# A shared ring of three PSUM bank pairs for attention scores and their maxima

## The reference

```python
x = x + attention(layernorm(x))          # x: 2 x 512 x 512, 32 heads of 16
scores = q @ k.T / sqrt(16)              # 64 (batch, head) pairs of 512 x 512
out = softmax(scores) @ v                # per head
attention = concat(out) @ w_o.T
x = x + experts(layernorm(x))            # top 2 of 8 experts, 512 -> 800 -> 512
```

## Time and profile before

| | us |
|---|---|
| median of three runs | 637.14 (635.68 to 637.60) |
| the profiled execution | 642.03 |
| its span, first to last instruction | 640.30 |
| QKV projection and start, of the span | 0 to about 98 |
| attention steps 0 to 15 and the last PV | about 98 to 291 |
| rest of the output projection, norm, router, experts | about 291 to 640 |

### The profile page before, as it was taken

How to read it: one execution, slowest core, us unless ns; L and a number is a source line. 1 busy time by engine, 2 the same in 40 slices (tenths; PEclk the granted TensorE clock), 3 DMA queues, 4 the chain that set the end, 5 groups by cost and what they waited for, 6 DMA issues and landing times.

```text
span 640.3 us, 10494 instructions
## 1 busy us (share of the span) xinstructions
PE 587.1 (92%) x3585; PEld 434.8 (68%) x3585; DVE 385.6 (60%) x689; ACT 329.5 (51%) x481; POOL 121.0 (19%) x137
## 2 busy tenths in 40 slices
PE   2999999979999999999954999999999999998993
PEld 2886663334333333323753999999999999998982
DVE  6715657958999999614546682837465555647140
ACT  5222116846777777862215464737464646565330
POOL 5000111000101101101004003324150607060312
PEclk9899997968999999999855999999999999999898
DMA  8180336764756620043742555666666574843213
GB/s 316 61 98 1 50 50 84 107 70 71 99 69 93 85 79 18 13 150 116 303 179 70 212 182 160 180 203 165 213 161 228 108 282 76 312 70 120 25 14 38
DMA packets 29497, 78.88 MB, mean 123 GB/s; under 512 B 8490, under 2 KB 8746, under 8 KB 24859
## 3 DMA queue, kind: packets, MB, share of 16 engines
q1 hardware_dynamic: 24474, 68.84, 40.0%
q0 software_dynamic: 4992, 9.64, 8.8%
HBM read 58.64 MB, written 9.80 MB: 107 GB/s over the span
## 4 chain that ended last, share of the span: by engine, by line
PE 45%; issue 28%; POOL 9%; DVE 7%; ACT 4%; DMA 3%; SPq 2%; POOLq 1%; ACTq 0%
PE ps_o L590 9%; PE ps L609 6%; PE ps L578 5%; PE ps L579 4%; PE ps L580 4%; DVE neg_max L1106 4%; POOL out L540 4%; PE ps L665 3%; PE ps_m L609 3%; POOL xn L522 3%; PE ps L621 2%; PE ps_o L729 2%; ACT probs_t L934 2%; SPq L357 1%; DMA rec_row<-sum_rec 1%
## 5 line engine op out<-in xcount | busy, mean ns | idle before, releaser
L934 ACT ACTIVATE probs_t<-ps 128x1024 f32<-128x1024 f32 x128 | 124.0, 1023 | 44.4 <-PE ps L621 43.1
L578 PE MATMUL ps<-xgT_hi,w_hi 128*128 128x294 f32 (+1 forms) x416 | 127.0, 305 | 5.4 <-DVE xgT_lo L1282 2.9
L580 PE MATMUL ps<-xgT_hi,w_lo 128*128 128x294 f32 (+1 forms) x416 | 126.3, 304 | 0.0
L579 PE MATMUL ps<-xgT_lo,w_hi 128*128 128x294 f32 (+1 forms) x416 | 125.5, 302 | 0.0
L1106 DVE TENSOR_REDUCE neg_max<-ps 128x1 f32<-128x512 f32 x171 | 111.7, 684 | 13.5 <-PE ps L609 11.4
L1295 DVE TENSOR_TENSOR act<-gate,ps 128x294 f32<-128x294 f32 x48 | 22.1, 461 | 105.4 <-PE ps L580 86.8
L578 PEld LDWEIGHTS ps<-xgT_hi,w_hi 128*128 128x128 f32 (+1 forms) x416 | 79.0, 190 | 5.9 <-DVE xgT_lo L1282 3.2
L579 PEld LDWEIGHTS ps<-xgT_lo,w_hi 128*128 128x128 f32 (+1 forms) x416 | 78.7, 189 | 0.0
L580 PEld LDWEIGHTS ps<-xgT_hi,w_lo 128*128 128x128 f32 (+1 forms) x416 | 78.4, 188 | 0.0
L609 PE MATMUL ps<-k_stack,q_stack 48*128 48x512 f32 x171 | 74.9, 479 | 2.9 <-issue 0.3
L590 PE MATMUL ps_o<-probs_t,v_ones 128*32 128x512 f32 x512 | 72.3, 639 | 0.3 <-ACT probs_t L934 0.3
(11 more groups left out here) (249 smaller groups left out, 960.2 us busy)
## 6 DMA issues: line engine op xcount, KB each, us to landing
w_sb<-w SPq DMA_DIRECT2D x18, 1024.0 KB
w_sb<-w SPq DMA_DIRECT2D x9, 1536.0 KB
w_sb<-w SPq DMA_DIRECT2D x9, 1152.0 KB
q_stack<-q_hi SPq DMA_DIRECT2D x32, 128.0 KB, 5.1
k_stack<-k_hi SPq DMA_DIRECT2D x32, 128.0 KB, 4.8
q_stack<-q_lo SPq DMA_DIRECT2D x16, 128.0 KB, 4.9
k_stack<-k_lo SPq DMA_DIRECT2D x16, 128.0 KB, 5.9
q_hi<-o_norm SPq DMA_DIRECT2D x16, 128.0 KB, 2.9
```

Source lines behind the costliest of these rows:

```text
L578: pe.matmul(o, x_hi, w_hi, start=start, stop=False)
L579: pe.matmul(o, x_hi, w_lo, start=False, stop=False)
L580: return pe.matmul(o, x_lo, w_hi, start=False, stop=stop)
L934: a.activation(probs_t[:, kc % 2, 2 * half:2 * half + 2, :], ps4[:, 2 * (n % 2):2 * (n % 2) + 2, :], ACT.Exp, scale=D ** -0.5).then_inc(s_ ...
```

## The change

- The six banks of `ps4` and `ps2` become one tensor `ps6`. Scores and maxima take bank pairs from it in turn: unit 2p of the scores, pair 2p of the maxima, unit 2p + 1, pair 2p + 1, each the next of the three pairs. An item waits for what stood in its pair before: scores for a maximum instruction, maxima for an exponential (`banks_free`).
- A maximum takes two banks: two matmuls (one in each row half), one semaphore increment, one DVE instruction over 128x1024 that writes two columns. There are eight for each group (PAIRS) in place of 16.
- PE's order in a quarter is now: score unit 2p, maxima pair 2p, in p = 1 the transpose (into `ps_m`), PV chunk, score unit 2p + 1, maxima pair 2p + 1. The PV chunk of a quarter is the same as before.
- `probs_t` becomes a ring of five units (PROBS). ACT copies the transposed maxima and `ps_o` both at u = 3.
- The raw output goes to `o_all` by DMA right after the sums. The reciprocals are spread by two DMAs of POOL's queue (to `rec_row`, four rows; then broadcast to 64 partitions of `rec_all`), and POOL multiplies in `o_all`, once for two groups. The stream shuffle is gone, as are the `rec_row` DMA on SP and `o_norm`.
- In steps 14 and 15 the scores use the pairs 0 and 2 of `ps6` alternately, and the projection tile is spread over the four quarters, one chunk after each.
- In the QKV projection one pair of maxima stands after most jobs and two pairs after every fourth; the jobs of the second batch use four banks in turn in place of five.

```diff
-        early = [divmod(n, 4 * TPB) for n in range(8 * TPB)]
-        between = [[early.pop(0) for _ in range(0 if n < TPB - 1 else 2 + n % 2) if early] for n in range(nj)]
+        early = [divmod(n, PAIRS) for n in range(2 * PAIRS)]
+        between = [[early.pop(0) for _ in range(0 if n < TPB - 1 else 1 + (n % TPB == TPB - 1)) if early]
+                   for n in range(nj)]
...
+        at = 0
+        for s in range(NG):
+            for p in range(TPB):
+                for half in range(2):
+                    both = [("scores", s, 2 * p + half)] + [("maxima", s + 2, 2 * p + half)] * (s + 2 < NG)
+                    for item in both:
+                        if s + 2 < NG:
+                            turns += [(item, (at, at + 1))]
+                        else:
+                            turns += [(item, (2 * half, 2 * half + 1))]
+                        at = (at + 2) % LAP
+                    if (p, half) == (1, 0) and s + 1 < NG:
+                        turns += [(("top", s + 1), (LAP,))]
...
+        def banks_free(eng, *item):
+
+            for kind, *at in held[item]:
+                if kind == "scores":
+                    eng.wait_ge(s_ex, UNITS * at[0] + at[1] + 1)
+                elif kind == "maxima":
+                    eng.wait_ge(s_mx, PAIRS * at[0] + at[1] + 1)
...
+            pool.wait_ge(s_init, 16 * SUBS)
+            pool.wait_ge(s_rows, 16)
+            for pair in range(NG // 2):
+                for r in range(2):
+                    g = 2 * pair + r
+                    pool.wait_ge(s_rc, g + 1)
+                    if g >= 1:
+                        pool.wait_ge(s_sh[(g - 1) % 2], 16 * ((g - 1) // 2 + 1))
+                    pool.dma_start(rec_row[:, :], sum_rec[:, r, :]).then_inc(s_rb, 16)
+                    pool.wait_ge(s_rb, 16 * (g + 1))
+                    if pair >= 1:
+                        pool.wait_ge(s_on, pair)
+                    pool.dma_start(rec_all[64 * r:64 * r + 64, :],
+                                   rec_row[:, :].unsqueeze(1).broadcast_to([GH, D, S])).then_inc(s_sh[r], 16)
+                for r in range(2):
+                    pool.wait_ge(s_oc[r], 16 * (pair + 1))
+                    pool.wait_ge(s_sh[r], 16 * (pair + 1))
+                pool.tensor_tensor(o_all[:, pair, :], o_all[:, pair, :], rec_all[:, :], ALU.mult).then_inc(s_on, 1)
...
-            def key_max(g, u2):
+            def key_max(g, m):
 
                 if g >= NG:
                     return
-                j, qt, _ = scores_at(u2)
-                q, k = head_at(g, j, ROWS)
-                max_bank_free(pe, g, u2)
-                pe.matmul(max_bank(g, u2), q[:, qt * P:(qt + 1) * P], k, start=True, stop=True).then_inc(s_sn, 1)
+                j, qt, _ = heads_at(m)
+                banks_free(pe, "maxima", g, m)
+                for par in range(2):
+                    q, k = head_at(g, j + par, ROWS)
+                    last = pe.matmul(banks_at("maxima", g, m)[:, par, :], q[:, qt * P:(qt + 1) * P], k,
+                                     start=True, stop=True)
+                last.then_inc(s_sn, 1)
...
                 for p in range(TPB):
-                    key_max(ga, 4 * p)
-                    key_max(ga, 4 * p + 1)
+                    scores(s, 2 * p)
+                    key_max(ga, 2 * p)
+                    if p == 1 and s + 1 < NG:
+                        max_t(s + 1)
                     if p < 2:
                         pv(s - 1, p + 2)
                     else:
                         pv(s, p - 2)
-                    if p == 0 and 0 <= s + 1 < NG:
-                        max_t(s + 1)
-                    key_max(ga, 4 * p + 2)
-                    scores(s, 2 * p)
-                    key_max(ga, 4 * p + 3)
                     scores(s, 2 * p + 1)
-                    if s in (NG - 2, NG - 1) and p == 1:
-                        projection(s - (NG - 2))
+                    key_max(ga, 2 * p + 1)
+                    if s in (NG - 2, NG - 1):
+                        projection(s - (NG - 2), p, p + 1)
...
-                v.tensor_reduce(neg_max[:, g % 2, col:col + 1], max_bank(g, u2), AX.X, ALU.max,
+                v.tensor_reduce(neg_max[:, g % 2, cols], banks_at("maxima", g, m), AX.X, ALU.max,
                                 negate=True).then_inc(s_mx, 1)
...
-                    if u2 == 11 and g >= 0:
-                        v.wait_ge(s_rb, 16 * (g + 1))
-                        if g >= 1:
-                            v.wait_ge(s_on, g)
-                        v.stream_shuffle(rec_all[:, :], rec_row[:, :], [1] * 32).then_inc(s_sh, 1)
```

More of the change, by code:

```diff
@@ L20 @@
 ROWS = PROD * D
+PROBS = 5
 HALF = 64
 RING = 4
+PAIRS = UNITS
+LAP = 6
 ROW = 98
@@ L213, in moe_layer @@
         s_rb = sem("s_rb")
-        s_sh = sem("s_sh")
+        s_sh = [sem(f"s_sh{r}") for r in range(2)]
         s_on = sem("s_on")
@@ L273, in head_at @@
             return [t[at][row:row + rows, slot, :] for t in (qs, ks)]
-        def scores_at(u2):
-            pair, par = divmod(u2, 2)
-            slot, qt = divmod(pair, TPB)
-            return 2 * slot + par, qt, par * 2 * TPB + slot * TPB + qt
-        turns = []
-        for s in range(-2, NG):
-            turns += [(s + 2, u2) for u2 in range(2)]
-            turns += [(s + 1, "maxima")] * (s + 1 >= 0)
-            turns += [(s + 2, u2) for u2 in range(2, 4 * TPB)]
-        turns = [t for t in turns if t[0] < NG]
@@ L290, in moe_layer, with heads_at @@
-        turns += [(t, "projection") for t in range(TPB)] + [(t, "router") for t in range(NT)]
-        max_banks = [ps2[:, 0, :], ps2[:, 1, :], ps_m[:, :]]
-        turn_of = {t: n for n, t in enumerate(turns)}
+        def heads_at(m):
+            slot, qt = divmod(m, TPB)
+            return 2 * slot, qt, slice(m, m + 2 * TPB + 1, 2 * TPB)
+        turns, at = [], 0
+        for g, m in [j for n in range(nj) for j in between[n]]:
+            if (g, m) == (1, 1):
+                turns += [(("top", 0), (at,))]
+                at = (at + 2) % 4
+            turns += [(("maxima", g, m), (at, at + 1))]
+            at = (at + 2) % 4
@@ new lines, in moe_layer, with bank_at @@
+        turns += [(("projection", t), ((6, 4)[t % 2],)) for t in range(2, TPB)]
+        turns += [(("projection", t), (t - TPB,)) for t in range(TPB, NT)]
+        turns += [(("router", t), ((5, 6, 4)[t % 3],)) for t in range(NT)]
+        banks_of, held, last_in = {}, {}, {}
+        for item, at in turns:
+            banks_of[item] = at
+            held[item] = [last_in[k] for k in at if k in last_in]
+            last_in.update({k: item for k in at})
+        def bank_at(*item):
+            return banks[banks_of[item][0]]
@@ L1126, in _ @@
                 if b == 1:
-                    for g, u2 in between[n - nj]:
-                        maximum(g, u2)
+                    for g, m in between[n - nj]:
+                        maximum(g, m)
             def residual(t):
```

148 lines of the change are left out of this document (65 added, 83 removed).

## The result

The changed kernel takes 666.25 us (median of four, 662.02 to 668.66), the one before 636.42 beside it (635.68 to 637.60). The ratio is 1.0438, with an interval of 1.0385 to 1.0490: slower by about 4%, or 29.8 us. The direction was forecast; the size was not (645.7, range 635 to 660).

A forecast was written before the change was run, and what follows sets the result against it. A loop of waits through PE's fixed order (PV, maximum, DVE, maximum, PV) was taken as the bound. Terms +10.4 + 1.4 - 2.2 - 1.0 = +8.6 us gave 650.6 profiled, 645.7 median; range 635 to 660.

The forecast's parts named there:

- The bound now, and the kind of the new one: Attention steps: a loop of waits through PE's order, 2.70 us a quarter before, another closed loop of 3.09 after.
- Rival A: Attention steps: exponential not in the way, DVE sets a step of 9.3 us; 601.6 us in all, chance 0.11.
- C: Attention quarters: PE's waits released sooner, quarter about 2.90 us, time 636 us, so no change; chance 0.12.
- the release of the exponential: Loop of each attention quarter: from the exponential's end to PE going on, put at 0.05 us.
- the 4.9 us taken off for the trace: Whole kernel: the profiled execution lay 4.9 us above its median, so 650.6 became a median of 645.7.
- The loop's sum: Attention quarter: 0.42 + 1.00 + 0.60 + 1.07 = 3.09 us; with the transpose, steps 1 to 13 last 163.7 us.
- The stall of 1.5 us: Start of step 3: the row of maxima comes late behind step 1's stack transfers; 1.5 us charged, bounds 0 and 8.6.
- Steps 14 and 15: Last two attention steps: quarters of 2.75 us with one projection chunk each; -2.2 us, bounds -4 and 0.
- The start: Between the QKV jobs: 16 pairs of maxima take 16 slots instead of 20; -1.0 us, bounds -1.5 and 0.
- Step 0: First attention step: 13.8 us from about 98.1, first PV of step 1 later by 1.4 us, bounds -2 and +3.
- Normalising, "so nothing": Normalising on POOL: no cost, with over a step of slack mid-way and 3 us more against about 8 of cover.
- Rival B: Attention steps: PE's idle time makes the clock fall again and again; 39 us more, 685 us, chance 0.11.

The follow-up runs named there:

- the half exponential: The changed kernel with each exponential over 512 of its 1024 elements, the first half's probabilities used for both: 664.82 us.
- before again: The kernel before the change, run unchanged for a second trace: 637.58 us, span 635.8 us.
- the move of PV: The changed kernel with the PV chunk put ahead of maxima pair 2p in PE's list instead of behind it: 667.63 us.

## Why the prediction was right and wrong

**The bound now, and the kind of the new one: right.** A closed loop through PE's fixed order, with PV in it, gave the pace before and gives it after. Rival A fell (halving the maximum changes nothing), and so did C (3.20 us a quarter, not 2.90).

The mechanism was right, and the 20.6 us between forecast and result are mostly three terms of the sum: the release of the exponential, counted 52 times (5.6 us), the normalising, which was put at nothing (4.3), and the 4.9 us taken off for the trace. One by one:

**The loop's sum: right in its parts, short in one.** Four of five terms came as written. The release of the exponential was put at 0.05, from the earlier trace rows, and was 0.15. The row that was read is a weight load behind an exponential in a run of four, PEld; in the loop it is PE's first matmul that counts (186.86 against the end at 186.71), and the weight load itself comes at 186.82. So each quarter is 0.11 us longer (3.20 against 3.09), and the transpose 0.2, about as taken: thirteen steps last 169.3 us (from the PV at 112.46 to that at 281.77) in place of 163.7, and 5.6 is the largest miss of the sum. The 641 to 655 named 0.05 a quarter as its uncertainty; a term that occurs 52 times had to be bounded by its own row.

**The stall of 1.5 us: wrong, nothing.** The step that failed is "end near 137.5, where step 3 would begin at about 136". SP issued the row of maxima at 129.28, 2.0 us after the last of the twelve stack transfers, and the first score unit of step 3 started at 136.86 without a wait, so the row was there by then. Two things were off by a little: the step began 0.9 later than assumed and the row was ahead of the estimate by at least 0.6. A difference of two estimates, each good to a microsecond, was charged at 1.5. The wait itself is real: PE waits 3.54 us for this row in the half exponential, 2.4 and 2.2 in the two kernels with the old ring and without the shuffle. As far as these runs tell, the step of 13.0 us kept it away here.

**Steps 14 and 15: the term was too small.** A chunk was taken as 3.70 / 4 = 0.90; alone between other matmuls it takes 1.06. Eight quarters of 2.90 in place of 2.75 are 1.2 us, and -2.2 became -1.1 (24.9 us to the end of the last PV, in place of 26.0).

**The start: -1.0 did not come.** PE waits 1.52 us at 98.53 for the DVE maximum of the last early pair, since the first score unit now shares its banks. The first PV of step 1 is at 112.46, 1.9 later than before, where +1.4 - 1.0 was forecast: 1.5 short. Step 0 itself, 13.9 us from its first unit, was right for that trace, and by luck: in others it is longer.

**Normalising, "so nothing": wrong.** Three things failed in it. The allowance of 3 us for two DMAs was far below one broadcast of 7; the row that was at hand, the transfer of the earlier trace rows, took 7.8 us from issue to use and should have been the upper bound. The cover of 8 us was counted for one group, where POOL's list has two in series, 20.5 us, and began them 6.9 us late. And "over a step of slack in the middle" is the time until a result is needed, not the time that POOL has for a group: its list is nearly full at steps of 13.0 us (78.2 of 78.3), and at the end it falls behind, as the last sums come 9.8 us apart (290.19, 300.13, 309.86) and POOL needs 11.4 us for a group (284.47 to 307.31 for two). The price is 7.5 us against before again: 5.0 of waiting, 2.0 of low clock behind it, and small differences. Against the trace of before it is only 4.3, since there the router ran at the low clock, which cost it about 3 us. The page of the Trainium skill that was cited there (DMA: Bandwidth & Descriptors, Latency and other measured facts) bears on the first byte only; by it the two would add an estimated 1.4 us, and the trace shows 2.5 for the small transfer alone and 7.0 to 7.3 for the broadcast.

Together: 5.6 (loop) - 1.5 (stall) + 1.1 (last steps) + 1.5 (start) + 4.3 (tail) + 0.3 (around the span) = 11.3 of the 11.4 us.

**Rival B: wrong for the steps, partly right for the start.** PE is idle for 0.83 and 0.78 us in each quarter, and the clock stays at 1.00 in the windows of the regular steps. The Trainium skill (TensorE: Matmul & The Clock Gate, A second HAM failure mode: psum-queue depth-cycling) would have the clock swing here, which was rival B's 685 us; the trace doesn't agree for the regular steps. What does happen is that the low clock at the start of attention can last longer in the ring: to 108, 112, 116 or 126 us, where it ends at 106 to 108 in the six traces of the old list. The prediction had no term for a spread of this size; its 13.8 us for step 0 fit the shortest of these starts.

**From trace to median.** The 4.9 us that the trace of before lay above its median were subtracted as if the changed kernel would keep them. Against before again, 1.6 of them came of the stop in steps 2 and 3, which the change removes, and 3.2 of the tail, where that execution had its router at the low clock; the traces of the changed kernel don't have it there. Without that subtraction the forecast is 650.6.

## What to carry to other kernels

When buffers of two producers become one ring, write down for each item which one it waits for and what stands ahead of it in every engine's list: the loop that closes sets the pace, and moving a long item only moves it to another loop, as the move of PV shows. When a step is given to an engine that waits for its own transfers, add up its whole list for a period, landings included, and compare it with the period that you hope for, not with the one that you have. And look at the irregular steps first: the 10 us gained here came from two long steps and one block of matmuls, with no new structure.

## What of the hardware was not expected

- A DMA that spreads four partitions of `rec_row` over 64 of `rec_all` (128 KB) takes 7.0 to 7.3 us from issue to use in the quiet tail and about 8.5 amid the stack transfers (190.37 to 198.85), on POOL's queue and on SP's alike (6.8); for half the bytes 4.4, once 5.3. The `q_hi<-o_raw` transfer, of the same 128 KB but from 64 partitions, has a median of 2.9 us in the same kernel. While the broadcast runs alone (322 to 326 us) the mean busy share of the 16 DMA engines is 0.25 at 27 GB/s, as much as four engines busy all the time would give; in 308.6 to 309.6, with `q_hi<-o_raw` under way, it is 0.77 at 206 GB/s. So it is likely that the four source rows leave the broadcast four engines. Another pattern was not tried.
- One DVE maximum over 1024 elements takes 1226 ns, against 684 for 512, and 692 for 512 in two halves of two banks; an exponential takes 1022 ns for 1024 and 597 for 512.
- The granted clock stayed at its upper level with PE idle for a quarter of every 3.2 us, but once it was low at the start of attention it took between 6 and 27 us to rise; with the same program 6 (101 to 107) and 14 (98.5 to 112). The low clock also comes and goes in the router: the same 32 matmuls take 3.8 or 6.8 us.
